# Local attention of the windowed layers in 64-query blocks of 96 keys, couples of head pairs, values laid out by transfers

## The reference, cut to what matters

```python
bk2, bv2 = look(bk), look(bv)            # each window of 32 keys with the window before it
mask = (it < jb) | (it > jb + w) | (jb == -1)
sim = jnp.einsum('bhwie,bhwje->bhwij', bq, bk2) * QK_SCALE
sim = jnp.where(mask, -jnp.finfo(sim.dtype).max, sim)
attn = jax.nn.softmax(sim, -1)
out = jnp.einsum('bhwij,bhwje->bhwie', attn, bv2)
```

## Time and profile before

| what | us |
|---|---|
| median of three runs | 6041.95 |
| the profiled execution | 6046.58 |
| its span, first to last instruction | 6044.8 |
| PE busy | 5374.6 |
| DVE busy | 4235.2 |
| ACT busy | 3913.8 |
| POOL busy | 2701.1 |

### The profile page before, as it was taken

One profiled execution on the slowest core, in us unless ns is written; L12 is line 12 of the kernel. 1 busy time (PEld: TensorE's weight loads), 2 busy tenths in 40 slices (PEclk: granted clock), 3 DMA queues, 4 the chain that ended last, 5 costly groups with the idle time before them and its releaser, 6 DMA issues. The chain is left out here.

```text
span 6044.8 us, 121573 instructions
## 1 busy us (share of the span) xinstructions
PE 5374.6 (89%) x41154; PEld 3795.8 (63%) x41154; DVE 4235.2 (70%) x16128; ACT 3913.8 (65%) x11510; POOL 2701.1 (45%) x2580
## 2 busy tenths in 40 slices
PE   7885799999999999997499999999999999697989
PEld 5674466666666666665256666666666666464678
DVE  4453788888888888885488888888888887454522
ACT  2211588888888888884178888888888888222333
POOL 0000556566565665652166566565565655230000
PEclk9996899999999999998599999999999999697999
DMA  0000000000000000000000000000000000000000
GB/s 11 22 1 3 22 1 12 9 12 9 5 12 6 12 9 12 8 1 4 21 1 11 8 3 12 9 12 9 7 10 6 12 8 1 5 2 4 2 29 8
DMA packets 30964, 53.45 MB, mean 9 GB/s; under 512 B 7688, under 2 KB 17168, under 8 KB 29712
## 3 DMA queue, kind: packets, MB, share of 16 engines
q1 hardware_dynamic: 30352, 45.66, 2.4%
HBM read 44.60 MB, written 1.05 MB: 8 GB/s over the span
## 5 line engine op out<-in xcount | busy, mean ns | idle before, releaser
L1791 PE MATMUL bank<-wA,next_rowT 128*128 128x512 f32 x2304 | 1217.0, 630 | 206.7 <-DVE turnB L2141 88.6
L1995 ACT ACTIVATE pairs<-pairs,negmax 128x128 f32<-128x128 f32 (+1 forms) x3072 | 1236.9, 418 | 8.0 <-DVE negmax L2102 7.0
L1972 POOL TENSOR_TENSOR turnA<-raw,ropes 128x512 f32<-128x512 f32 x768 | 969.1, 1272 | 152.6 <-ACT raw L2019 123.8
L2102 DVE CUSTOM_DVE_ANT_0 pairs<-bank,bands,big 128x128 f32<-128x128 f32 (+1 forms) x3072 | 940.6, 362 | 62.9 <-PE bank L1720 59.4
L1979 POOL TENSOR_TENSOR qk<-turnA,turnB 128x512 f32<-128x512 f32 x768 | 976.4, 1272 | 6.4 <-DVE turnB L2141 6.4
L1951 POOL COPY spread<-recip 128x256 f32<-128x256 f32 x768 | 305.6, 398 | 1262.7 <-DVE recip L2111 1256.9
L1791 PEld LDWEIGHTS bank<-wA,next_rowT 128*128 128x128 f32 x2304 | 370.8, 191 | 689.1 <-DVE turnB L2141 286.3
L2002 ACT ACTIVATE pairsT<-bank 128x512 f32<-128x512 f32 x768 | 465.9, 607 | 303.7 <-PE bank L1733 303.4
L1995 ACT ACTIVATION_READ_ACCUMULATOR pairs<-pairs,negmax 128x1 f32 x3072 | 624.7, 203 | 0.0
L285 POOL TENSOR_TENSOR rstd<-vareps,neg_half 128x2 f32<-128x2 f32 x56 | 39.0, 696 | 1288.4 <-DVE vareps L256 892.3
L2141 DVE TENSOR_TENSOR turnB<-bank,ropes 128x512 f32<-128x512 f32 x768 | 522.4, 680 | 0.0
(11 more groups left out here) (313 smaller groups left out, 11261.8 us busy)
## 6 DMA issues: line engine op xcount, KB each, us to landing
wA<-in_wt_wqkv SPq DMA_DIRECT2D x72, 256.0 KB, 2.8
wB<-in_wt_wo SPq DMA_DIRECT2D x12, 512.0 KB, 3.5
wC<-in_wt_w SPq DMA_DIRECT2D x12, 341.0 KB, 2.9
wD<-in_wt_w SPq DMA_DIRECT2D x12, 192.0 KB, 2.3
big<-in_e_up SPq DMA_DIRECT2D x1, 2048.0 KB
big<-in_e_down SPq DMA_DIRECT2D x1, 2048.0 KB
scl<-in_wt_scales SPq DMA_DIRECT2D x12, 128.0 KB, 3.3
X<-in_x SPq DMA_DIRECT2D x8, 128.0 KB, 2.3
```

Source lines behind the costliest of these rows:

```text
L1791: pe.matmul(side_bank(i)[:, :], c.next_rowT[:, t * P:(t + 1) * P], wqkv[:, k * 512:(k + 1) * 512], start=True, stop=True).then_inc(s.chunk ...
L1972: g.tensor_tensor(c.turnA[:, m % 2, :].rearrange("p (h d) -> p h d", h=8), c.raw[:, m % 4, :].rearrange("p (h d) -> p h d", h=8), cos, ALU ...
L1995: last = a.activation(tile, tile, ACT.Exp, scale=-1.0, bias=c.negmax[:, 2 * p + side, t:t + 1], accum_out=c.pair_sums[:, p % 4, t, side:si ...
L2102: last = v.tensor_tensor_reduce(c.pairs[:, 2 * (p % 4) + side, AT[t]:AT[t] + SPAN[t]], c.bank[side][:, AT[t]:AT[t] + SPAN[t]], c.bands[:, ...
```

## The change

Queries are taken in blocks of 64 with the 96 keys that they can see, so no block needs a corner of its neighbour. Work goes by couples of pairs (n = 0 to 3). `pe_scores` makes 16 products of 64 queries with 96 (at the sequence's start 64) keys, in four tiles: the sides in row tiles, the blocks in column tiles. Minima and exponentials are 96 wide. `pe_turn_probs` turns four blocks of 128x96 a pair, in one of two banks. `pe_weigh` has the turned probabilities stationary and the values moving, 16 products of 64x64 over 96 keys, and leaves the context in token order; `dve_scale_ctx` divides there with one product of 512 columns, `pe_turn_ctx` turns it, `act_copy_ctx` copies it. POOL's spread, the turned shares and the turned corner go away. The values of each block of 96 keys must lie on partitions 0 to 95, so SP copies V to `values` by three transfers for each half of the heads (`sp_values`), and V has one buffer. Probabilities of the first pair of a turn are turned at the end of slot 7 before. SP's list of weight loads is written out turn by turn between these transfers, with the same waits. The mask comes from memory. POOL's list is otherwise as it was.

```diff
-DVE_RSQRT_SLOTS = {2: 0, 6: 1}
+DVE_RSQRT_SLOTS = {3: 0, 6: 1}
...
+        def pe_scores(pe, T, n):
             j = T % 2
...
+            pe.wait_ge(s.qT_copied, T * 4 + n + 1)
+            pe.wait_ge(s.kT_copied, T * 4 + n + 1)
+            if T > T0 or n > 0:
+                pe.wait_ge(s.negmax_ready, T * PAIRS + 2 * n)
+            for e in range(2):
+                for t in range(HALVES):
+                    for w in range(2):
+                        q0 = t * P + w * BLOCK
+                        k0 = max(q0 - WINDOW, 0)
+                        keys = q0 + BLOCK - k0
+                        at = (2 * e + t + 1) * BLOCK_KEYS - keys
+                        for side in range(2):
+                            q, k = [x[j][DH * side:DH * side + DH, 2 * n + e, :] for x in (qT, kT)]
+                            last = pe.matmul(c.bank[side][w * BLOCK:(w + 1) * BLOCK, at:at + keys], q[:, q0:q0 + BLOCK],
+                                             k[:, k0:k0 + keys], start=True, stop=True, skip_group_check=True)
             last.then_inc(s.scores_ready, 1)
...
+        def pe_weigh(pe, T, n):
+            pe.wait_ge(s.probsT_ready, T * PAIRS + 2 * n + 2)
+            pe.wait_ge(values_laid[n // 2], VALUE_PARTS * (T + 1))
+            if T > T0 or n > 0:
+                pe.wait_ge(s.ctx_ready, T * COUPLES + n)
+            for e in range(2):
+                for t in range(HALVES):
+                    for side in range(2):
+                        at = ((2 * e + t) * 2 + side) * DH
+                        for w in range(2):
+                            turned = c.probsT[0:BLOCK_KEYS, e, (2 * side + t) * P + w * BLOCK:(2 * side + t) * P + (w + 1) * BLOCK]
+                            last = pe.matmul(c.bank[4][w * BLOCK:(w + 1) * BLOCK, at:at + DH], turned,
+                                             values[n // 2][0:BLOCK_KEYS, 2 * t + w, 4 * (n % 2) + 2 * e + side, :],
+                                             start=True, stop=True, skip_group_check=True)
             last.then_inc(s.ctx_in_psum, 1)
+        def pe_turn_ctx(pe, T, n):
+            pe.wait_ge(s.ctx_scaled, T * COUPLES + n + 1)
+            for m in range(4):
+                last = pe.transpose(c.bank[4][:, m * P:(m + 1) * P], scaled[:, m * P:(m + 1) * P], c.ident[:, :])
+            last.then_inc(s.ctxT_in_psum, 1)
...
         def pe_window(pe, T):
             following = has_turn(T + 1)
...
+            for slot in range(PAIRS):
+                n = slot // 2
+                if slot % 2 == 0:
+                    pe_turn_probs(pe, T, slot + 1)
+                    if n >= 1:
+                        pe_turn_ctx(pe, T, n - 1)
+                    elif has_turn(T - 1):
+                        pe_turn_ctx(pe, T - 1, COUPLES - 1)
+                    if slot == 0 and following:
+                        pe_xT(pe, T + 1)
+                    if slot == 6 and has_turn(T - 2):
+                        pe_gates(pe, T - 2, (s.qT_copied, (T + 1) * 4 + (1 if following else 0)))
+                    if n + 1 < COUPLES:
+                        pe_scores(pe, T, n + 1)
+                    elif following:
+                        pe_scores(pe, T + 1, 0)
+                else:
+                    pe_weigh(pe, T, n)
+                for i in PE_LATE_QKT_SLOTS.get(slot, ()):
                     pe_turn_qk(pe, T, i)
...
+                if slot == 1 and has_turn(T - 3):
                     pe_ff_out(pe, T - 3)
...
+                if slot == 2 and has_turn(T - 2):
                     pe_shift(pe, T - 2)
...
+                if slot == 6 and has_turn(T - 1):
                     pe_out(pe, T - 1, (s.kT_copied, (T + 1) * 4 + (1 if following else 0)))
...
+                if slot == 7 and has_turn(T - 2):
                     pe_linear(pe, T - 2)
                 if following:
...
+                    pe_prepare(pe, T + 1, slot, False)
+                if slot == 5 and has_turn(T - 2):
                     pe_turn_normed(pe, T - 2)
+                if slot % 2 == 1 and n + 1 < COUPLES:
+                    pe_turn_probs(pe, T, slot + 1)
+                elif slot % 2 == 1 and following:
+                    pe_turn_probs(pe, T + 1, 0)
...
+        def act_copy_ctx(a, T, n):
+            a.wait_ge(s.ctxT_in_psum, T * COUPLES + n + 1)
+            a.activation(part_of(ctxT[T % 2], n), c.bank[4][:, :], ACT.Identity).then_inc(s.ctx_ready, 1)
...
         def act_window(a, T):
             following = has_turn(T + 1)
...
+            for slot in range(PAIRS):
+                n = slot // 2
                 if following:
...
+                    for i in ACT_CHUNK_SLOTS.get(slot, ()):
                         act_copy_chunk(a, T + 1, i)
...
+                    if slot == 6:
                         act_copy_q(a, T + 1, 0)
...
+                if slot % 2 == 0:
+                    act_copy_probs(a, T, slot)
+                    act_copy_probs(a, T, slot + 1)
+                    if slot == 0 and following:
+                        act_xT(a, T + 1)
+                    if n >= 1:
+                        act_copy_ctx(a, T, n - 1)
+                    elif has_turn(T - 1):
+                        act_copy_ctx(a, T - 1, COUPLES - 1)
+                    if slot == 6 and has_turn(T - 2):
+                        act_normedT(a, T - 2)
+                    if slot == 0:
+                        act_copy_q(a, T, COPY_LATE_QKT_SLOTS[slot])
+                    if slot == 6 and has_turn(T - 2):
                         act_gelu(a, T - 2)
...
+                if slot == 3:
+                    act_copy_q(a, T, COPY_LATE_QKT_SLOTS[slot])
+                p = slot + 2
+                if p < PAIRS:
...
+        def dve_scale_ctx(v, T, n):
+            v.wait_ge(s.recip_ready, T * COUPLES + n + 1)
+            v.wait_ge(s.ctx_in_psum, T * COUPLES + n + 1)
+            shares = c.recip[:, 0, 8 * (n % 2):8 * (n % 2) + 8].unsqueeze(2).broadcast_to((P, 8, DH))
+            v.tensor_tensor(scaled[:, :].rearrange("p (n d) -> p n d", n=8), c.bank[4][:, :].rearrange("p (n d) -> p n d", n=8),
+                            shares, ALU.mult).then_inc(s.ctx_scaled, 1)
...
         def dve_window(v, T):
             following = has_turn(T + 1)
...
+            for slot in range(PAIRS):
+                n = slot // 2
+                if slot == 6 and following:
                     dve_copy_k(v, T + 1, 0)
...
+                if slot == 7 and has_turn(T - 1):
                     dve_add(v, T - 1)
...
+                if slot % 2 == 0:
+                    dve_recip(v, T, n)
+                if following:
+                    for m in DVE_ROTATE_SLOTS.get(slot, ()):
+                        dve_rotate(v, T + 1, m)
+                if slot == 3:
+                    dve_copy_k(v, T, COPY_LATE_QKT_SLOTS[slot])
+                if slot % 2 == 0:
+                    for e in range(2):
+                        if n + 1 < COUPLES:
+                            dve_negmax(v, T, 2 * n + 2 + e)
+                        elif following:
+                            dve_negmax(v, T + 1, e)
+                else:
+                    dve_scale_ctx(v, T, n)
+                if slot == 0:
+                    dve_copy_k(v, T, COPY_LATE_QKT_SLOTS[slot])
+                if slot == 1 and has_turn(T - 3):
+                    dve_ff_add(v, T - 3)
+                if slot == 7 and has_turn(T - 2):
                     dve_last_hidden(v, T - 2)
...
+                if slot == 3 and has_turn(T - 2):
                     dve_ff_stats(v, T - 2)
                 if following:
...
+                    dve_prepare(v, T + 1, slot)
+                elif slot == 3:
                     dve_roots(v, ss[:, ff_var], rs[(T + 1) % 2][:, ff_var])
...
+                if slot == 4 and has_turn(T - 2):
                     dve_ff_normalise(v, T - 2, rs[(T + 1) % 2][:, ff_var])
...
+                if slot == 7:
                     if has_turn(T - 2):
                         dve_first_hidden(v, T - 2)
...
+        def sp_values(sp, q, part):
+            sp.wait_ge(s.chunk_copied, q * N_CHUNKS + (6, 12)[part])
+            if q > T0:
+                sp.wait_ge(s.ctx_in_psum, q * COUPLES - (2, 0)[part])
+            src, out, done = V[:, :, 8 * part:8 * part + 8, :], values[part], values_laid[part]
+            sp.dma_start(out[WINDOW:BLOCK_KEYS, 0:4:2, :, :], src[0:BLOCK, :, :, :]).then_inc(done, 16)
+            sp.dma_start(out[0:BLOCK_KEYS, 1:4:2, :, :], src[WINDOW:P, :, :, :]).then_inc(done, 16)
+            sp.dma_start(out[0:WINDOW, 2, :, :], src[P - WINDOW:P, 0, :, :]).then_inc(done, 16)
```

More of the change, by code:

```diff
@@ L1726, in pe_turn_probs @@
             pe.wait_ge(s.probs_ready, T * PAIRS + p + 1)
-            if T * PAIRS + p > T0 * PAIRS:
-                pe.wait_ge(s.probsT_ready, T * PAIRS + p)
-            for side in range(2):
-                probs, out = c.pairs[:, 2 * (p % 4) + side, :], c.bank[2][:, S * side:S * side + S]
-                pe.transpose(out[:, 0:P], probs[:, 0:P], c.ident[:, :])
```

(6 more changed lines are left out.)

327 lines of the change are left out of this document (121 added, 206 removed).

## The result

| kernel | median us | range of runs | profiled run | its span |
|---|---|---|---|---|
| before | 6041.61 | 6040.45 to 6043.06 | 6046.58 | 6044.8 |
| changed | 6322.69 | 6316.82 to 6325.23 | 6320.73 | 6319.0 |

The changed kernel takes 1.0464 times as long, 95% interval 1.0446 to 1.0482: 281 us slower, against a forecast of 6310 (+268). First the busy times on the page of the changed kernel: PE has less to do (5374.6 us before), DVE 486 us less (4235.2), and the span is longer all the same.

A forecast was written before the change was run, and what follows sets the result against it. A chain that changes engine, mainly between DVE and PE, bounds each turn. From 44.63 to 47.3 us over 92 turns, +244, clock +20, less 4.6, on 6046.6 gives 6306, stated as 6310; range 6000 to 6560.

The forecast's parts named there:

- The mechanism: Slots 3 and 4: statistics and roots behind DVE's key copy make the rotations late; PE idles 3.0 us.
- The forecast's idles: PE waits 3.0 us in slot 4, 2.2 in slot 5 and 1.3 ahead of slot 6's gates.
- PE's saving: Scores and weighing: a couple costs 2.1 us where two pairs cost 2.86, so PE saves 3.0 us a turn.
- Four tiles at once: A couple's scores on PE: matmuls in four tiles run together, 0.66 us, about 0.96 with form and way back.
- two tiles at once: Rival on PE's scores: 1.32 us a couple, 49.3 us a turn, 6475 us; chance 0.17, shared with a half clock.
- The rival that this saving goes through: Roots off the chain: 41.6 us a turn, 5770 us, if rotation 4 ends before PE's slot 4 work, 22.1; chance 0.15.
- A term mis-sized: the statistics: DVE's row statistics in slot 3, behind key copy and product, were taken at 2.09 us.
- The other mis-sized term: the clock: PE at half clock behind the idles of slots 4 and 5: 0.2 us a turn, between zero and 1.7; +20 us.
- Slot 5's account: ACT's exponentials of pair 6 delay the copies of slot 5's projections, so reduction and rotation; PE idles 2.2 us.
- The covers: Transfers of V, some 5 us each, have over 20 us before weighing reads them: zero cost.
- The setup: Before the turns, POOL's selects are traded for a load: -2 to +3 us, taken as zero.

The follow-up runs named there:

- b1: The kernel before, with only DVE's row statistics and first roots moved from slot 2 to slot 3, behind the key copy; attention unchanged: 6329.7 us.
- c1: The changed kernel with another order on PE, DVE and ACT, same work: gates behind scores, statistics back in slot 2, roots still in slot 3, among others: 5772.8 us.
- d4: c1 with one piece put back: DVE's row statistics in slot 3, behind the key copy and the product: 5979.1 us.
- e1: The changed kernel with DVE's row statistics and first roots back at the end of slot 2: 6248.5 us.
- e2: The changed kernel with extra PE work in its two idles: slot 4's scores and slot 5's weighing each computed three times: 6263.7 us.
- e5: The changed kernel with two moves undone: statistics and roots at the end of slot 2, gates behind the scores in slot 6: 6187.2 us.
- e3: The changed kernel with ACT's exponentials of pair 6 behind its copies of slot 5's two projections: 6258.5 us.
- d5: c1 with one piece put back: DVE's minima and normalised rows ahead of the rotations in slots 4 and 5, ACT's exponentials ahead of the copies: 6005.3 us.
- v1: The changed kernel with the transfers of the values cut to one head in eight, same number of transfers and waits: 6324.6 us.

## Why the prediction was right

**The mechanism.** That statistics and roots, moved behind the key copy, put the rotations of slot 4 on the end was the main step. b1 shows it apart from the rest of the change. The two don't weigh alike: c1 leaves the roots behind the copy and PE idles 1.07 us in slot 4, d4 puts the statistics there too and it idles 1.95. The forecast's idles were 3.0 (slot 4), 2.2 (slot 5) and 1.3 us (gates); measured at full clock: 2.02, 2.11 and 1.23. The turn was to take 47.3 us and takes 47.18 where the clock costs nothing.

**PE's saving.** Four tiles at once: 0.82 us for a couple's scores, where I had 0.96 with the change of form and the way back; two tiles at once would have shown 1.3 or more. Weighing 1.08 against 1.13. From start to next start a couple costs 1.90 against 2 x 1.33 for two old pairs, 3.0 us a turn as forecast, and PE's busy time in a turn falls by some 3.2 (c1). The rival that this saving goes through (5770) fell in the changed kernel. c1 takes 5772.8, but not by that rival's condition: rotation 4 still holds PE up by 1.07 us, and other idles are closed, so the nearness of the two numbers is chance.

**A term mis-sized: the statistics.** I carried over 2.09 us from the earlier trace rows, where they start at 2018.64 and end at 2020.73. At their new place they take 1.01 (2066.06 to 2067.07). One instruction of the five makes the difference, by the statistics of its line (count, shortest, median and longest ns), first in the kernel before, then in b1, where it is the same line:

```profile
L2205 DVE TENSOR_SCALAR big<-big x96: 168/1254/1267, 769.9 to 5178.5; 128x2 f32<-128x2 f32 x96
```

```profile
L2205 DVE TENSOR_SCALAR big<-big x96: 169/170/170, 781.3 to 5464.7; 128x2 f32<-128x2 f32 x96
```

In the kernel before POOL adds beside it:

```profile
2019.40 1.26 POOL L1979 TENSOR_TENSOR qk<-turnA,turnB 128x512 f32<-128x512 f32 x1
```

```profile
2019.45 1.25 DVE L2205 TENSOR_SCALAR big<-big 128x2 f32<-128x2 f32 x1
```

In b1 POOL is idle there, and the instruction takes 0.17. So slot 4's idle came out at 2.02 and not 3.0, and a duration read beside other work was not the instruction's own. The Trainium skill has this on its page "SBUF — State Buffer", section "Who interferes with whom": VectorE and GpSimd share a pair of ports, and `tensor_scalar` is among the VectorE instructions that can take it, where whoever issues first holds it to its end and the other fully blocks. The trace agrees, with 1.25 us here and 1.22 in e1.

**The other mis-sized term: the clock.** I took 0.2 us a turn, between zero and 1.7; e2 shows 0.58, and other orders pay more: 0.9 in e1, 1.3 in d4, 1.6 in e5. Where it counts was right: behind slot 4's idle for nothing (the turn of 47.18 holds such a stretch, and only its idle in slot 5 shrinks), behind slot 5's on the chain (48.45). I had no row on how often it falls; it falls in each of the 88 turns, behind one of the two idles.

**The sum.** Of the 1.1 us that the statistics don't take, 0.5 are left at the end of rotation 4, since the key copy starts 18.2 us behind the start of slot 0 (2046.62) and not 17.75; slots 4 to 7 then take 0.4 more than I had, so the turn without the clock is 0.12 short. The clock is 0.38 over. That makes 3.13 us a turn against 2.87 forecast (47.3 - 44.63, and 0.2), over 88 whole turns where I counted 92: 276 against 264. So the nearness of the whole, 13 us, is in part luck: errors of up to 1.1 us a turn went against each other.

**Slot 5's account was half right.** I put its idle down to ACT's exponentials. e3 shows that DVE's minima and normalised rows stand right behind them: ACT's order alone left 1.53 us of 2.11. c1 changes both orders and the idle goes, d5 puts both back and it returns; DVE's order alone was not run.

**The covers held.** The bytes of the transfers cost nothing (v1), and weighing never waited for them, as forecast. The setup, which I took as zero without a row, costs nothing either: outside the whole turns the profiled spans hold 2116.9 us before and 2115.6 after.

What stays open: what decides in which of the two places the clock falls in a turn. The runs show where and at what price, not why there.

## What to carry to other kernels

Price a moved instruction by what is late next on its engine, not by its length: the same statistics and roots cost 3.1 us a turn more behind a copy that waits for PE than ahead of it (b1). Before giving up on a change that takes work off the busiest engine and is slower, put the order right around it, all idles together: single repairs here gave 64 to 92 us, the whole 550. And where an engine idles in every turn, look at the clock behind the idle; work put into the idle can be worth more than nothing.
